# Three elementwise sums of a GRU and RK4 time loop are issued by GpSimd instead of VectorE

## The reference

```
def cell(h, x):                       # GRU
    r, z = sigmoid(i_r + h_r), sigmoid(i_z + h_z)     # i = x @ W_ih + b_ih, h_ = h @ W_hh + b_hh
    n = tanh(i_n + r * h_n)
    return (1 - z) * n + z * h
x = x + GRU outputs                   # the sum x1
def derivative(q, p):                 # RK4, four stages s = 0..3 in a step, DT = 0.01
    dq = q - q**3/3 - p + x + tanh(q) @ coupling.T + bias
    dp = 0.08 * (q + 0.7 - 0.8 * p)
q, p = clip(rk4_step(q, p), -20, 20)
out = x + q                           # the output's sum
```

## Time and profile before

| what | us |
|---|---|
| median of 3 runs (lowest, highest) | 1103.17 (1100.84, 1103.2) |
| the profiled execution's own time | 1101.07 |
| its span | 1099.2 |
| TensorE busy, matmul | 972.0 (88%) |
| VectorE busy, 2726 instructions | 996.9 (91%) |
| ScalarE busy, 1485 instructions | 590.8 (54%) |
| GpSimd busy, 16 instructions | 9.5 (1%) |
| mean granted TensorE clock, as a share of full | 0.967 |

### The profile page before, as it was taken

The page is one execution under the profiler, slowest core; times in us unless marked ns, Lnnn a source line. Parts: engine busy times, 40 slices in busy tenths (PEclk is TensorE's granted clock), DMA queues, the critical chain, the costliest instruction groups (busy, mean ns, idle before and its releaser), DMA issues.

```text
span 1099.2 us, 54943 instructions
## 1 busy us (share of the span) xinstructions
PE 972.0 (88%) x23809; PEld 943.0 (86%) x23809; DVE 996.9 (91%) x2726; ACT 590.8 (54%) x1485; POOL 9.5 (1%) x16
## 2 busy tenths in 40 slices
PE   6699999999989999799998999899999999998674
PEld 6699999899889998799987898889889999998674
DVE  5779999999979999799997999889999999999988
ACT  5645555555545555455554555445555555554442
POOL 2000000000000000000000000000000000000000
PEclk9899999999989999899998999989999999998788
DMA  8001010101101101001101001101001100000000
GB/s 335 11 13 32 18 32 32 33 18 32 32 19 32 32 18 32 27 24 32 33 17 33 29 20 32 33 18 32 30 19 32 37 13 22 22 23 13 21 13 12
DMA packets 29334, 35.91 MB, mean 33 GB/s; under 512 B 3616, under 2 KB 27936, under 8 KB 28960
## 3 DMA queue, kind: packets, MB, share of 16 engines
q1 hardware_dynamic: 29088, 32.27, 9.0%
HBM read 23.87 MB, written 8.39 MB: 29 GB/s over the span
## 4 chain that ended last, share of the span: by engine, by line
DVE 46%; PE 22%; ACT 15%; issue 14%; DMA 1%; DVEq 1%; SPq 0%; ACTq 0%; POOL 0%
PE ps_rk L286 13%; DVE q L549 7%; PE ps_rz L286 6%; DVE ps_rk L549 5%; ACT th_hi L457 5%; ACT th L453 5%; DVE cube L693 4%; DVE th_lo L549 4%; DVE b_mid L549 4%; DVE base L552 4%; ACT rz L433 4%; PE ps_gi L325 3%; DVE n_in L549 3%; DVE drive L549 2%; DVE h_lo L549 2%
## 5 line engine op out<-in xcount | busy, mean ns | idle before, releaser
L286 PE MATMUL ps_rk<-th_hi,cpl_lo 128*128 128x64 f16 x4096 | 166.5, 195 | 102.6 <-ACT th_hi L457 84.0
L286 PEld LDWEIGHTS ps_rk<-th_hi,cpl_lo 128*128 128x128 f16 x4096 | 137.8, 99 | 130.4 <-issue 72.8
L453 ACT ACTIVATE th<-q 128x256 f32<-128x256 f32 x256 | 106.2, 415 | 222.9 <-DVE q L549 221.6
L325 PE MATMUL ps_gi<-xs_hi,wih_hi 128*128 128x256 f32 x744 | 223.1, 300 | 1.7 <-ACT gi L416 1.7
L325 PE MATMUL ps_gi<-xs_lo,wih_hi 128*128 128x256 f32 x744 | 212.8, 286 | 0.0
L325 PE MATMUL ps_gi<-xs_hi,wih_lo 128*128 128x256 f32 x744 | 212.4, 286 | 0.0
L286 PE MATMUL ps_rk<-th_lo,cpl_hi 128*128 128x64 f16 x4096 | 167.7, 196 | 4.4 <-issue 4.4
L286 PE MATMUL ps_rk<-th_hi,cpl_hi 128*128 128x64 f16 x4096 | 165.8, 195 | 0.0
L325 PEld LDWEIGHTS ps_gi<-xs_hi,wih_hi 128*128 128x128 f32 x744 | 145.1, 195 | 2.1 <-ACT gi L416 2.1
L286 PEld LDWEIGHTS ps_rk<-th_lo,cpl_hi 128*128 128x128 f16 x4096 | 142.7, 100 | 4.8 <-issue 4.8
L325 PEld LDWEIGHTS ps_gi<-xs_lo,wih_hi 128*128 128x128 f32 x744 | 145.3, 195 | 0.0
(11 more groups left out here) (118 smaller groups left out, 1637.2 us busy)
## 6 DMA issues: line engine op xcount, KB each, us to landing
ring<-x_in SPq DMA_DIRECT2D x64, 128.0 KB, 2.2
out<-ring SPq DMA_DIRECT2D x64, 128.0 KB, 1.8
xs_raw<-x_in SPq DMA_DIRECT2D x60, 128.0 KB, 2.1
gi<-wih_in SPq DMA_DIRECT2D x4, 768.0 KB, 7.1
whh_raw<-whh_in SPq DMA_DIRECT2D x4, 768.0 KB, 9.8
cpl_raw<-cpl_in SPq DMA_DIRECT2D x1, 1024.0 KB, 14.0
q<-cond_in SPq DMA_DIRECT2D x1, 128.0 KB, 6.3
h<-cond_in SPq DMA_DIRECT2D x1, 128.0 KB, 6.7
```

The costliest lines, as they stand in the source:

```text
L286: mm = nc.tensor.matmul(ps[:, m * B:(m + 1) * B], w[:, k, w_cols + m * P:w_cols + (m + 1) * P], v[:, k * B:(k + 1) * B], start=False, stop ...
L325: last = nc.tensor.matmul(ps_gi[i][:, 0:CHUNK * B].rearrange("p (j b) -> p j b", j=CHUNK), w[:, k, m * P:(m + 1) * P], v[:, :, k, :], star ...
L453: nc.scalar.activation(th[:, :], q[:, s, :], ACT.Tanh).then_inc(th_ready, 1)
```

## The change

The three sums leave VectorE's list and become `tensor_tensor` instructions in GpSimd's. GpSimd gets `over_steps` of its own: in each step it issues `add_out(t0, j-1)`, `cell_x1(t0, j+1)` and `split_x_lo(t0, j+10)` in that order, each behind the semaphores that it had, and the counts that they raise (`out_ready`, `x1_ready`, `xs_lo_ready`) are the same. `clip_q` on VectorE gets one more wait, for `out_ready`, since it overwrites the q that `add_out` of the step before reads. VectorE's one wait for `xs_lo_ready` ahead of the steps goes. A lower clamp of two magnitudes changes from 2^-100 to 2^-60.

```
-            def cell_x1(t0, u):
-                dve.wait_ge(x_loaded[u % SLOTS], rounds(t0, u))
-                dve.wait_ge(h_ready, t0 + (u + 1))
-                tt(ring[:, u % SLOTS, :], ring[:, u % SLOTS, :], h[:, :], ALU.add, x1_ready)
...
-            def split_x_lo(t0, u):
-                dve.wait_ge(xs_hi_ready, t0 + (u + 1))
-                half = u // CHUNK % 2
-                tt(xs_lo[half][:, u % CHUNK, :, :].rearrange("p k b -> p (k b)"), xs_raw[:, u % SLOTS, :],
-                   xs_hi[half][:, u % CHUNK, :, :].rearrange("p k b -> p (k b)").bitcast(F32), ALU.subtract, xs_lo_ready)
...
             def clip_q(t0, j):
                 dve.wait_ge(q_raw_ready, t0 + (j + 1))
+                wait(dve, out_ready, t0 + j)
                 nc.vector.tensor_scalar(q[:, 0, :], q_raw[:, :], -CLAMP, CLAMP, op0=ALU.max, op1=ALU.min).then_inc(q_ready, 1)
...
-            def add_out(t0, j):
-                dve.wait_ge(q_ready, t0 * 4 + (4 * j + 4))
-                tt(ring[:, j % SLOTS, :], ring[:, j % SLOTS, :], q[:, 0, :], ALU.add, out_ready)
...
         @block.gpsimd
         def _(pool):
...
+            def cell_x1(t0, u):
+                pool.wait_ge(x_loaded[u % SLOTS], rounds(t0, u))
+                pool.wait_ge(h_ready, t0 + (u + 1))
+                nc.gpsimd.tensor_tensor(ring[:, u % SLOTS, :], ring[:, u % SLOTS, :], h[:, :],
+                                        ALU.add).then_inc(x1_ready, 1)
+
+            def add_out(t0, j):
+                pool.wait_ge(q_ready, t0 * 4 + (4 * j + 4))
+                nc.gpsimd.tensor_tensor(ring[:, j % SLOTS, :], ring[:, j % SLOTS, :], q[:, 0, :],
+                                        ALU.add).then_inc(out_ready, 1)
...
+            cell_x1(0, 0)
+
+            def step(t0, j):
+                if not isinstance(t0, int) or t0 + j >= 1:
+                    add_out(t0, j - 1)
+                if before(t0, j + 1, T):
+                    cell_x1(t0, j + 1)
+                if splits_x(t0, j):
+                    split_x_lo(t0, j + AHEAD)
+            over_steps(pool, step)
+            add_out(T - SLOTS, SLOTS - 1)
```

More of the change, by code:

```diff
@@ L633, in _ @@
             dve.wait_ge(allmags_ready, 1)
-            nc.vector.tensor_scalar(mags[:, MAG_WHH:MAG_WHH + 1], allmags[:, MAG_WHH:MAG_WHH + 1], 2.0 ** -100, None,
+            nc.vector.tensor_scalar(mags[:, MAG_WHH:MAG_WHH + 1], allmags[:, MAG_WHH:MAG_WHH + 1], 2.0 ** -60, None,
                                     op0=ALU.max).then_inc(whh_scaling, 1)
@@ L661, in _ @@
             dve.wait_ge(allmags_ready, 2)
-            nc.vector.tensor_scalar(mags[:, MAG_CPL:MAG_CPL + 1], allmags[:, MAG_CPL:MAG_CPL + 1], 2.0 ** -100, None,
+            nc.vector.tensor_scalar(mags[:, MAG_CPL:MAG_CPL + 1], allmags[:, MAG_CPL:MAG_CPL + 1], 2.0 ** -60, None,
                                     op0=ALU.max).then_inc(cpl_scaling, 1)
@@ L788, in _ @@
             dve.wait_ge(cpl_scaling, 14)
-            cell_x1(0, 0)
             cell_drive(0, 0)
@@ L793, in _ @@
             split_cpl_lo(3)
-            dve.wait_ge(xs_lo_ready, AHEAD)
             def step(t0, j):
@@ L798, in step @@
                 stage_y(t0, j, 0)
-                if not isinstance(t0, int) or t0 + j >= 1:
-                    add_out(t0, j - 1)
                 split_tanh_lo(t0, j, 0)
@@ L832, in step @@
                 stage_cube(t0, j, 2)
-                if more_cells:
-                    cell_x1(t0, j + 1)
                 stage_base(t0, j, 2)
@@ L849, in step @@
                     start_e(t0, j + 1)
-                if splits_x(t0, j):
-                    split_x_lo(t0, j + AHEAD)
                 stage_q(t0, j, 3)
@@ L854, in _, with split_x_lo @@
             over_steps(dve, step)
-            add_out(T - SLOTS, SLOTS - 1)
         @block.gpsimd
         def _(pool):
-            def split_x_lo(u):
-                pool.wait_ge(xs_hi_ready, u + 1)
+            def split_x_lo(t0, u):
+                pool.wait_ge(xs_hi_ready, t0 + (u + 1))
                 half = u // CHUNK % 2
-                src = ring if u < SLOTS else xs_raw
+                src = ring if isinstance(t0, int) and t0 + u < SLOTS else xs_raw
                 nc.gpsimd.tensor_tensor(xs_lo[half][:, u % CHUNK, :, :].rearrange("p k b -> p (k b)"), src[:, u % SLOTS, :],
@@ L865, in split_x_lo @@
                                         ALU.subtract).then_inc(xs_lo_ready, 1)
+            def cell_x1(t0, u):
[7 more added lines that the diff above has]
+                                        ALU.add).then_inc(out_ready, 1)
             for u in range(2 * CHUNK):
-                split_x_lo(u)
+                split_x_lo(0, u)
             pool.wait_ge(mags_ready, 1)
```

## The result

The changed kernel takes 1113.11 us in the median (1111.23 to 1114.7), against 1103.18 us before. The ratio is 1.0095, with a 95% interval of 1.0073 to 1.0117: slower by 10 us, where I forecast 59 more and a range that began at 1120. The sign was right, the size was six times too large. An instruction that is held up though its queue has reached it is said to stand.

The account below looks back on a forecast made before the run. VectorE's stretch from `th_lo` to the third `stage_q` was taken to bound each step. Two blocked turns of 0.60 us less a 0.12 us gain, over the steps with edge corrections, gave +60.8 us: 1162 us, range 1120 to 1186.

Parts of the forecast that it names:

- What bounds the kernel: VectorE leads from `th_lo` of stage 0 to the third `stage_q`; only work taken from there shortens the step.
- GpSimd gets its turn though VectorE has the next instruction at hand, and VectorE loses 0.60 us for each turn: Read from the setup: GpSimd's sum breaks in between queued VectorE instructions over the shared port, costing 0.60 us each time.
- `cell_x1`, +0.60 us: GpSimd's x1 sum gets in at the end of `base`, `q_sum` stands, and the step grows by 0.60 us.
- the first rival: Little or no blocking; GpSimd runs beside VectorE or where it idles or reads PSUM: 1080 to 1104, chance 0.10.
- the second rival: One blocked turn per step, not two, as either sum finds a gap: 1129, with 1115 to 1140 around it, chance 0.11.
- `split_x_lo`, +0.60 us: GpSimd's `xs_lo` sum makes `ps_rk` or `cube` stand ahead of the third `stage_q`, adding 0.60 us.
- `add_out`, nothing: The output's sum falls where VectorE waits before `th_lo`: no cost, 0.1 us as upper end.
- The gain of 0.12 us: Removing x1 between `cube` and `base` shortens that stretch from 1.00 to 0.88 us; a full pitch, 0.33 us, the other end.
- The sum: 54 steps with two blocked turns, nine with x1 alone, less back-edges, plus exposed sums: +60.8 us.
- Back-edges: At four loop back-edges VectorE stands some 3 us, hiding the first blocked turn: -2.4 us.
- The clock: TensorE's granted clock stays near 1.00 in the loop; the rival that it falls meant 1210, chance 0.07.
- The signs that I had named: Trace after: `q_sum` about 1.0 us, `ps_rk` or `cube` likewise, VectorE busy time not falling, loop step 16.9 us.

Follow-up runs that it names:

- e6: Changed kernel with `xs_lo` back on VectorE and the second `y_sum` between `cube` and `base` of stage 2: 1080.36 us, ratio 0.9807.
- e8: Changed kernel with the second `y_sum` ahead of `base` of stage 2 and GpSimd's `xs_lo` also waiting for the third `stage_q`: 1083.58 us, ratio 0.9822.
- e2: Changed kernel with only the `xs_lo` sum on GpSimd, the other two back on VectorE: 1127.58 us, ratio 1.0223.
- e4: Changed kernel, all three sums on GpSimd, with the second `y_sum` moved between `cube` and `base` of stage 2: 1106.22 us, ratio 1.0035.
- e12: e2 with an added 8-column VectorE sum of two tiles between `cube` of stage 2 and x1: 1137.26 us.
- e1: Changed kernel with only the x1 sum on GpSimd, the other two back on VectorE: 1089.66 us, ratio 0.9884.
- e3: Changed kernel with only the output's sum on GpSimd, the other two back on VectorE: 1103.16 us, ratio 0.9999.
- e7: Kernel before the change with only the second `y_sum` moved ahead of `base` of stage 2: 1102.81 us, ratio 1.0004.
- e16: Changed kernel with three added 128x256 VectorE sums in the setup behind the fourth `wih_lo`: the three took 2.72 us; no kernel time given.
- e15: e2 with an added 1536-column VectorE sum of two tiles between `cube` of stage 2 and x1: 1267.69 us.
- e9: e2 with the `cube` of stage 2 taking its constant from a one-column tile, same values: 1129.41 us, ratio 1.0249.
- e10: e4 with `drive`'s scale taken from the instruction (1.0) instead of a tile, which changes the computation: 1077.73 us, ratio 0.9785.

## Why the prediction was wrong, point by point

- **What bounds the kernel.** Right. Steps without `xs_lo` are shorter after the change by 0.16 us and those with it are longer by what `base` stands, less that gain. Taking `xs_lo` off VectorE's list gave nothing by itself: e6, which leaves it there, is no slower than e8, which moves it.
- **"GpSimd gets its turn though VectorE has the next instruction at hand, and VectorE loses 0.60 us for each turn."** This is the step that failed. That the two exclude each other, and that GpSimd holds VectorE for 0.60 us from the end of the instruction that it waited for, was right in the traces of the runs above, in the setup and in the steps. That it gets the turn at the next boundary was taken from one place of the setup and is not so in the steps of the changed kernel: `q_sum` lasted 0.42 us and `cube` 0.42, and in e2 four boundaries passed. In the loop, VectorE's queue kept GpSimd out until it had a gap, read a scalar from a tile, or read PSUM. In straight parts of e4 and e8, and at the added sum of 8 columns in e12, it let GpSimd in without any of these, so the rule is not complete.
- **`cell_x1`, +0.60 us.** Measured: nothing, or 0.03 us in the straight parts. GpSimd ran beside `stage_q`. I had named this in the first rival ("got its turn only where VectorE is idle or reads PSUM") and gave it 0.10. For x1 it was the truth, and e1's 1089.66 lies in that rival's 1080 to 1104. For the two sums together the nearest was the second rival, one blocked turn and not two, which had 0.11; its 1115 to 1140 took that turn at 0.60 us and the gain at 0.12, where the trace has 0.41 and 0.20.
- **`split_x_lo`, +0.60 us.** Measured: +0.41 us, at `base`, an instruction that I had not listed. The gap in front of `base` is the one that the removal of x1 opened; I had counted it as a gain of 0.12 us and not asked who else would use it. With x1 left in place, e2, the cost is +0.48 us at `drive`.
- **`add_out`, nothing.** Right, by e3.
- **The gain of 0.12 us.** 0.20 us in e1. The earlier trace rows understated it: there `y_sum` started 0.43 us after `base`, in e1 0.34 us. The full pitch, 0.33 us, is to be had when another instruction fills the place (e6).
- **The sum.** By these prices a loop step is 0.41 - 0.20 = +0.21 us, which is the measured step. I had +1.08. Of the forecast 60.8 us the x1 term held 54 + 9 turns, 38 us, of which nothing came. That the sign is right all the same rests on `base`, which the prediction did not list, and is in part luck.
- **Back-edges.** I took 2.4 us off; the four together are 3.8 us longer, from -0.1 to +2.1 each. No run explains them. In e1 and e6 some of them are shorter and some longer, and in e7, whose time is that of before, the four are 3.1 us longer, so I count them as scatter of the profiled run.
- **The clock.** Right that it would hold: 0.965 after, 0.967 before.
- **The signs that I had named.** `cube` to `base` is 0.45 us and GpSimd's sums average over 0.72, as forecast. `q_sum`, `ps_rk` and `cube` did not stretch, VectorE's busy time fell, and a loop step is 16.03 us and not 16.9, so by them the price was wrong.

The lock that the Trainium skill describes (SBUF — State Buffer, "SBUF: two separate sides") is in these traces, at 0.60 us a turn and not the 0.72 of the whole sum. The page's order, that whoever starts first has the pair, fits the steps: a VectorE instruction that follows without a gap comes before a waiting GpSimd sum. It does not fit e16, nor the steps of e4 and e8 in which the waiting sum came first.

## What to carry to other kernels

A sum moved to GpSimd costs VectorE about 0.5 us where it gets in, so ask where that is: list VectorE's instructions behind the moment at which GpSimd's operands are ready, and look for the first dependent gap, scalar read from a tile, or PSUM operand. With the kernel's own instructions this list held in all loop steps here, but not in all straight ones (e4, e8), so read the durations in each part of the trace after. If the first such place is in the leading stretch, delay GpSimd's request to a place with slack, or fill the gap; here that turned +10 us into -19 to -22 us. And a price read from the setup of a kernel must be tried in the steady state before it is multiplied by 54.

## What the runs showed of the hardware

- GpSimd's 128x256 sum, once in, keeps a VectorE instruction with two SBUF operands out for 0.59 to 0.60 us from the end of the one before (after, e2); that instruction then lasts 0.94 to 0.96 us, or 0.83 us behind a gap of 0.03 us, and up to 0.99 us where GpSimd began first (e8).
- Between queued VectorE instructions of 128, 256 or 1536 columns in a loop step, GpSimd is passed over for up to 3.4 us (e15). In the straight parts it got in at such a boundary in 11 steps of e4 and 14 of e8, unexplained. A gap of 0.03 us (after, `base`) or the reading of one scalar column (e9, e10) is enough to let it in.
- A VectorE instruction that reads PSUM runs beside GpSimd's sum at its usual 0.48 us (the `q` at 614.98 after).
- An 8-column VectorE sum lets GpSimd in and then lasts 0.72 us (e12), and in the setup each boundary of the added sums does (e16: 0.9 us each); neither is explained.
